# A step's norm transposes and projections moved one step earlier, and the rotation with them

## What is computed

```
xn  = layernorm(x)
out = x + attn(xn) + ffn(xn)
attn: q, k, v = xn @ Wqkv; q and k rotated by position (16 heads of 8); scores plus a bias that
      falls with |i-j| (per head); causal softmax; times v; @ Wo
ffn:  n1 = layernorm(xn, w, b); rw = gating(n1)              (8 experts, at least 2 active)
      q, k, v = sum over e of rw[e] * (n1 @ proj[e]); causal softmax attention
      hs = xn + sum over e of rw[e] * (attention @ o_proj[e])
      n2 = layernorm(hs); rw2 = gating(n2)
      hs + sum over e of rw2[e] * (gelu(n2 @ w1[e]) @ w2[e])
```

## Time and profile before

| what | us |
|---|---|
| median of three runs | 1389.92 |
| the three runs | 1386.5 to 1391.0 |
| the profiled execution | 1386.97 |
| its span in the trace | 1385.1 |

### The profile page before, as it was taken

One profiled execution on the slowest core, in us unless ns is written; L12 is line 12 of the kernel. 1 busy time (PEld: TensorE's weight loads), 2 busy tenths in 40 slices (PEclk: granted clock), 3 DMA queues, 4 the chain that ended last, 5 costly groups with the idle time before them and its releaser, 6 DMA issues.

```text
span 1385.1 us, 33706 instructions
## 1 busy us (share of the span) xinstructions
PE 1229.1 (89%) x10780; PEld 938.4 (68%) x10780; DVE 1004.5 (73%) x3691; ACT 707.4 (51%) x1281; POOL 211.0 (15%) x325
## 2 busy tenths in 40 slices
PE   1249999999999999999999999999999979999998
PEld 0127777777777677777777777777777766777776
DVE  5547777777777777777777777777777657777653
ACT  1115555555555555555555555555555665555532
POOL 1011111121111222221111111112111200000000
PEclk9659999999999999999999999999999999999999
DMA  5312232222222222222322222222222106544344
GB/s 131 87 63 79 79 90 81 82 82 77 78 78 82 81 80 78 77 77 81 96 97 77 77 79 88 81 82 81 80 80 78 53 26 230 194 154 154 154 169 153
DMA packets 107942, 133.19 MB, mean 96 GB/s; under 512 B 18116, under 2 KB 87252, under 8 KB 99692
## 3 DMA queue, kind: packets, MB, share of 16 engines
q1 hardware_dynamic: 105668, 131.66, 29.6%
q10 hardware_dynamic: 2216, 0.80, 0.2%
HBM read 109.12 MB, written 21.54 MB: 94 GB/s over the span
## 4 chain that ended last, share of the span: by engine, by line
PE 68%; DVE 16%; issue 9%; SPq 4%; DMA 2%; ACT 1%; DVEq 0%; ACTq 0%
PE ps L1448 9%; PE ps L1493 9%; PE ps L1694 8%; PE ps L1449 8%; PE ps L1680 8%; PE ps L1321 4%; PE ps L1458 3%; PE ps L1425 2%; DVE mx L1070 2%; PE ps L1408 2%; SPq L415 2%; PE ps L1371 1%; PE ps L1507 1%; PE ps L1381 1%; DVE xn L894 1%
## 5 line engine op out<-in xcount | busy, mean ns | idle before, releaser
L1070 DVE TENSOR_REDUCE mx<-ps 128x4 f32<-128x1024 f32 (+1 forms) x192 | 234.9, 1223 | 89.4 <-PE ps L1381 80.0
L663 ACT ACTIVATE pr<-ps 128x1024 f32<-128x1024 f32 x192 | 195.8, 1020 | 138.4 <-PE ps L1408 93.7
L558 POOL TENSOR_TENSOR n1s<-rep,n1T 128x256 f32<-128x256 f32 x256 | 176.8, 728 | 254.3 <-DVE mpart L1084 254.3
L669 ACT ACTIVATE ps<-trn 128x1024 f32<-128x1024 bf16 x191 | 197.2, 1032 | 5.1
L1694 PEld LDWEIGHTS ps<-w2s,ats 128*128 128x128 f32 x1024 | 131.7, 192 | 49.8 <-issue 46.8
L1448 PE MATMUL ps<-n1s,wqk 128*128 128x256 f32 x512 | 163.0, 400 | 0.0
L1449 PE MATMUL ps<-n1s,wqk 128*128 128x256 f32 x512 | 152.7, 380 | 0.0
L1458 PE MATMUL ps<-wv,n1s 128*128 128x128 f32 x1024 | 141.6, 281 | 0.0
L1493 PE MATMUL ps<-wop,ats 128*128 128x128 f32 x1024 | 140.0, 294 | 0.0
L842 ACT ACTIVATE n1s<-ps 128x512 f32<-128x512 f32 x128 | 76.5, 597 | 122.6 <-PE ps L1680 121.5
L1694 PE MATMUL ps<-w2s,ats 128*128 128x128 f32 x1024 | 135.7, 276 | 0.5 <-DVE ats L1253 0.5
(11 more groups left out here) (228 smaller groups left out, 2038.3 us busy)
## 6 DMA issues: line engine op xcount, KB each, us to landing
rep<-scr_rw SPq DMA_DIRECT2D x32, 1024.0 KB, 5.0
stk<-scr_rw SPq DMA_DIRECT2D x16, 1024.0 KB, 8.1
stk<-scr_parts SPq DMA_DIRECT2D x896, 16.0 KB
scr_parts<-parts SPq DMA_DIRECT2D x64, 192.0 KB, 2.3
rots<-scr_rw SPq DMA_DIRECT2D x8, 1024.0 KB, 4.8
wqk<-scr_rw SPq DMA_DIRECT2D x8, 1024.0 KB, 8.9
stk<-scr_parts SPq DMA_DIRECT2D x128, 48.0 KB
xt<-in_x SPq DMA_DIRECT2D x32, 128.0 KB, 2.5
```

The lines of the kernel that those rows point to most:

```text
L558: pool.tensor_tensor(n1s[:, e], rep[:, par, e], n1T[:, par], ALU.mult).then_inc(n1s_done, 1)
L663: act.activation(pr[:, Q, :, i], ps[:, S2[0]:S2[0] + NF], ACT.Exp).then_inc(exp_done, 1)
L669: act.activation(ps[:, S2[0]:S2[0] + NF], seeds[:, kind:kind + 1].broadcast_to((P, NF, 512)), ACT.Copy).then_inc(seed_done, 1)
L1070: dve.tensor_reduce(mx[:, min(i, 1)].rearrange("p (f h) -> p f h", f=NF)[:, :, h:h + n], ps[:, S1[0]:S1[0] + NF].rearrange("p f (h t) -> p ...
```

## The change

Sequence n+3 instead of n+2 now gets its norm transposes, both projections and its rotation in step n, in the step's tail; sequence n+2's gating stays in step n. The transposes go into S1[0] (after the last `row_max`), the q projection into S1[1], the k projection into PVB (after `add_x` has read it). `weights_T` and `max_T` move to G1. On PE `unit1`(2) to `unit1`(5) each move one place forward. On DVE `rotate` stands between `add_x` and `add_hs`, and all six `row_max` stand beside gating links. On ACT `evac_norm` is split: xnT in the tail, n1T and its square at the head of the next step.

```diff
-GATE_MAX_AT = (7, 12, 17, 22)
+GATE_MAX_AT = (2, 7, 11, 16, 20, 24)
...
+        FIRST, LATER = (G0, G1, G1), (S1[0], S1[1], PVB)
...  ACT, step
                 if n_x >= 2:
-                    evac_norm(n + 2, u)
+                    evac_norm_1(n + 2, u, LATER)
...
                 if n_x >= 2:
+                    evac_v(n + 2, u)
+                if n_x == 3:
+                    evac_norm_x(n + 3, LATER)
+                if n_x >= 2:
                     evac_weights(n + 2)
-                    evac_v(n + 2, u)
...  DVE, step
                 def beside_gating(k):
                     next(norm, None)
                     if k in GATE_MAX_AT:
-                        next_max(2 + GATE_MAX_AT.index(k))
-                    if k == 11:
+                        next_max(GATE_MAX_AT.index(k))
+                    if k == 17:
+                        soft_max(n)
+                    if k == 18:
                         normalise(n, 0)
-                    if k == 14:
-                        soft_max(n)
-                    if k == 20:
+                    if k == 28:
                         soft_norm(n)
                 if n_x >= 2:
-                    rotate(n + 2, beside_rotation)
-                    next_max(1)
                     gating(n + 2, T, 0, gate1, LG1, NORM1, 1, beside_gating)
...
                 add_x(n, u)
+                if n_x == 3:
+                    rotate(n + 3, LATER)
                 add_hs(n, u)
...  PE, step
-                if n_x >= 2:
-                    norm_T(f, lambda: pe.wait_ge(ats_done, len(ATS_CHUNKS) * n))
                 unit2(n, u, 0)
                 qk(n, 0)
-                if n_x >= 2:
-                    proj(f, 0, lambda: pe.wait_ge(hs_done, n))
                 qk(n, 1)
...
                 if n_x >= 2:
-                    proj(f, 1, lambda: pe.wait_ge(rot_chain, ROT_LINKS * f + 1))
                     logits(f)
...
                 qk(n, 6)
+                next_max(2)
                 qk(n, 7)
-                pv(n, u, 0)
+                pv(n, u, 0, f if n_x >= 2 else None)
...
                 if n_x >= 2:
-                    weights_T(f, True)
                     proj_v(f, True)
+                if n_x == 3:
+                    norm_T(g, LATER, lambda: pe.wait_ge(s1_read, UNITS * f))
+                    proj(g, 0, LATER, lambda: None)
+                if n_x >= 2:
+                    weights_T(f, lambda: None)
                 if n_x:
                     max_T(n + 1)
                 att_T(n)
+                if n_x >= 2:
+                    pe.wait_ge(rwT_done, f + 1)
+                if n_x:
+                    pe.wait_ge(mT_done, n + 2)
                 oe(n, 0)
                 oe(n, 1)
                 att_out(n)
+                oe(n, 2)
+                oe(n, 3)
+                if n_x == 3:
+                    proj(g, 1, LATER, lambda: pe.wait_ge(xa_done, n + 1))
...
-                for e in range(2, E):
+                for e in range(4, E):
                     oe(n, e)
```

More of the change, by code:

```diff
@@ L609, in _, with evac_norm_x, evac_norm_1 @@
             act.activation(red[:], red[:], ACT.Sin).then_inc(set_act, 1)
-            def evac_norm(b, par):
+            def evac_norm_x(b, banks):
+                act.wait_ge(xzT_out, b + 1)
+                act.activation(xnT[:], ps[:, banks[0], 0:S], ACT.Copy).then_inc(xnT_done, 1)
+            def evac_norm_1(b, par, banks):
                 act.wait_ge(xzT_out, b + 1)
@@ L616, in evac_norm @@
                     act.wait_ge(n1s_done, E * (b - 1))
-                act.activation(xnT[:], ps[:, G0, 0:S], ACT.Copy).then_inc(xnT_done, 1)
-                act.activation(n1T[:, par], ps[:, G0, S:2 * S], ACT.Identity, bias=lnp[:, 1:2],
+                act.activation(n1T[:, par], ps[:, banks[0], S:2 * S], ACT.Identity, bias=lnp[:, 1:2],
                                scale=lnp[:, 0:1]).then_inc(n1T_done, 1)
@@ L813, in _ @@
             for b in range(2):
-                evac_norm(b, b)
+                evac_norm_x(b, FIRST)
+                evac_norm_1(b, b, FIRST)
                 evac_logits(b)
@@ L1312, in norm_T, with proj @@
                     for i in range(T):
-                        ins = pe.transpose(ps[:, G0, (T * k + i) * P:(T * k + i + 1) * P], src[:, i], ident[:])
+                        ins = pe.transpose(ps[:, banks[0], (T * k + i) * P:(T * k + i + 1) * P], src[:, i], ident[:])
                 ins.then_inc(xzT_out, 1)
-            def proj(b, side, prev):
+            def proj(b, side, banks, prev):
                 pe.wait_ge(xnT_done, b + 1)
@@ L1320, in proj @@
                 for k in range(2):
-                    ins = mm(ps[:, G1, k * S:(k + 1) * S], wa[:, 2 * side + k], xnT[:], start=True, stop=True)
+                    ins = mm(ps[:, banks[1 + side], k * S:(k + 1) * S], wa[:, 2 * side + k], xnT[:], start=True, stop=True)
                 ins.then_inc((rot_q_out, rot_k_out)[side], 1)
@@ L1345, in proj_v, with weights_T, unit1 @@
                 ins.then_inc(v_out, 1)
-            def weights_T(b, old):
+            def weights_T(b, free):
                 pe.wait_ge(rw_out, 3 * (b + 1))
[L1349 to L1354, removed]
+                free()
+                pe.transpose(ps[0:E * T, G1, 0:P], gt[:, 6, 0:T].rearrange("p i e -> p (i e)"), ident[:]
                              ).then_inc(rwT_out, 1)
-            def unit1(b, par, k):
+            def unit1(b, par, k, front=None):
                 Q, i = divmod(k, 3)
-                if k == 0:
-                    pe.wait_ge(rwT_done, b + 1 if not isinstance(b, int) or b else 2)
-                    pe.wait_ge(mT_done, b)
+                if k == 0 and front is not None:
+                    pe.wait_ge(n1T_done, front + 1)
+                    pe.wait_ge(rot_chain, ROT_LINKS * front + 1)
                 if i == 0:
@@ L1413, in unit2, with pv @@
                 ins.then_inc(s2_out, 1)
-            def pv(n, u, Q):
+            def pv(n, u, Q, front=None):
                 pe.wait_ge(exp_done, UNITS * n + 3 * (Q + 1))
@@ L1422, in pv @@
                     pe.wait_ge(xa_done, n)
+                    if front is not None:
+                        pe.wait_ge(rot_chain, ROT_LINKS * front + 3)
                 for f in range(NF):
@@ L1461, in ve, with soft_scores @@
                     ins.then_inc(ve_out, 1)
-            def soft_scores(n, free):
+            def soft_scores(n):
                 pe.wait_ge(qkT_done, 2 * (n + 1))
-                free()
+                pe.wait_ge(hs_done, n)
                 b = ps[:, G1]
@@ L1593, in step @@
                 qk(n, 6)
+                next_max(2)
                 qk(n, 7)
-                pv(n, u, 0)
+                pv(n, u, 0, f if n_x >= 2 else None)
                 if n_x == 0:
                     logits2(0)
-                next_max(2)
+                next_max(3)
                 unit2(n, u, 3)
-                soft_scores(n, (lambda: pe.wait_ge(rot_chain, ROT_LINKS * f + 3)) if n_x >= 2 else
-                            (lambda: pe.wait_ge(hs_done, n)))
+                soft_scores(n)
                 ve(n, 0)
```

52 lines of the change are left out of this document (28 added, 24 removed).

## The result

The changed kernel takes 1460.18 us at the median of four runs (1449.65 to 1475.48), the kernel before 1389.76: slower by a ratio of 1.0485, interval 1.0385 to 1.0585. The forecast was 1442 with a range of 1402 to 1464. The ratio is that of the other three runs, since the profiled execution, 1475.48, is over 1.5% longer than the shortest.

The account below looks back on a forecast made before the run. TensorE's queue was taken to set the pace. A step loses 4.3 us instead of 3.05, plus 0.1: 28 x 1.3 = 36; 1387 + 36 + 19 for the clock = 1442 us, range 1402 to 1464.

Parts of the forecast that it names:

- The main term: TensorE at unit1(1) loses 2.8 us a step through the late load of xt; u is the start of unit2(0).
- the loop: unit1(1), k projection, rotation, hs, bs, load of xt, statistics, row_max(0), unit1(1) again; nothing in it overlaps.
- What it takes away: TensorE's waits at weights_T, max_T, att_T, unit1(5) and nearly all of soft_T's go: up to 3.05 us a step.
- What it adds in the tail: Losses at the q projection (0.6), pv(1) (0.55), oe(0) (0.25) and soft_T (0.1): together 1.5 us a step.
- The rival with the early load: Load of xt isn't last, there when the gating starts: a step 0.95 us shorter, 1353 us; chance 0.11.
- The clock: TensorE's clock falls in three of four steps instead of nine of 28: 12 more falls at 1.55, 19 us.
- The landing: Load of xt, 128 KB, lands 2.5 us after issue by the trace, 2.3 by the Trainium skill; 2.5 used.

Follow-up runs that it names:

- The early load: Changed kernel with the load of xt for sequence n+3 issued at the head of SP's step, ahead of its wait for base_done: 1368.02 us, ratio 0.985.
- the swap: Changed kernel with xt's load ahead of xr's in SP's step, both still behind base_done: 1412.63 us, ratio 1.0179 to the kernel before.
- the place of the rotation: Changed kernel with the rotation behind add_hs instead of right behind add_x, SP's order unchanged: 1413.4 us, ratio 1.0165 to the kernel before.
- the place of row_max(0): Changed kernel, late load kept, with row_max(0) ahead of the layer norm's first piece: 1372.56 us, ratio 0.9887 to the kernel before.
- the run that fills it: Changed kernel with six extra unused 128x256 float matmuls in front of unit1(1): 1430.64 us, ratio 1.0294 to the kernel before.

## Why the prediction was right, and where it was off

The direction, the mechanism and the place were right, and the median lies inside the range, near its upper end. Of the 18 us by which it misses the forecast, 3 are the base (the prediction starts from the profiled 1387, not from the median) and 13 the short steps, if these are as long in the executions that have no trace. That leaves 2 for the clock, so the size of the miss is that of one term in the tail.

- *The main term.* u + 3.0 for base_done was measured as u + 3.0, the statistics at u + 6.7 (predicted 7.0), TensorE due at unit1(1) at u + 6.4 (6.4), started at u + 9.1 (9.2). The loss there was 2.6 to 2.9 (2.8) in the short steps. The early load, the swap, the place of the rotation and the place of row_max(0) each move it as the loop says.
- *What it takes away.* Right: nothing waits at weights_T, at max_T or for the softmax any more.
- *What it adds in the tail.* The q projection, 0.64 (0.6), and pv(1), 0.63 (0.55), were right. The first oe was mis-sized: 0.83 to 0.88, not 0.25. The step that failed is "oe(0) waits for ScalarE's mT, some 0.7 behind max_T, with 0.2 and 0.3 of work in front". ScalarE copies the weights first, and by the change that copy waits for max_T too (mT_out, since both lie in bank G1), so two copies stand in a row behind it:

```profile
847.66 0.27 ACT L649 ACTIVATE rwT<-ps 16x128 f32<-16x128 f32 x1 [1.52 <-PE ps L1396]
847.84 0.36 ACT L654 ACTIVATE mT<-ps 48x256 bf16<-48x256 bf16 x1
```

  The first oe starts 848.43 - 847.27 = 1.16 behind max_T, not 0.7: the copy of the weights is 0.18 of the difference, and 0.23 from the end of mT's copy to the start of oe had been left out. The work in front is 0.33 (max_T 0.11, att_T 0.22), not 0.5. With this term a step loses 4.85 instead of 4.3, and 28 x 1.75 = 49 took the place of 36.
- *The rival with the early load.* For the case that the load isn't last I had a step 0.95 shorter than before. The kernel with the early load shows none: 3.2 lost instead of 2.1, by the 0.6 at the first oe and because unit1(1) loses 0.94, not 0.6. What it gains comes from the clock: its steps average 0.57 less than before (some 16 of the 21 us), and the nine falls had cost 0.5 a step. That rival's 1353 would have been 1368.
- *The clock.* Three of four steps were forecast and 20 of 28 measured. No row of the kernel before gave three of four, so that the number came out is luck. The size did not, in the profiled execution: 1.55 for each was taken from the steps before, where the clock was low for 3.4 us; here it was low for 6.8 in twelve steps, and a long step is 2.8 above the short ones on the mean. Forecast for the clock: 19. Measured there: 20 x 2.8 less the 15 of before, 41, of which some 9 are late landings (an estimate from the step lengths above). With 49 for the short kind that makes 90, and the spans differ by 88.6. The medians differ by 70.4, which leaves some 21 beside the 49, close to the 19: that the total is near is in part this, since the median run had less of the low clock than the profiled one.
- *The landing.* The page of the profile shows 2.5 again for xt, and the mean idle in front of the statistics is 2.2 (predicted 2.2), but that is a mean of two kinds: on time it is 1.6 to 2.1 (2.4 from issue to statistics in the step shown), in thirteen of 28 steps 2.4 to 3.0. The prediction counted with one value in every step; the spread matters because each late landing went with a fall of the clock. The 2.3 by the Trainium skill (DMA: Bandwidth & Descriptors, "Anatomy of one DMA — SWDGE (gpsimd) path") and the trace's 2.5 could not be told apart by the total, beside the clock.

That the clock falls more often and for longer was shown to come from TensorE's wait at unit1(1) by the run that fills it. Of the twelve falls of 6.8 us, eleven are in steps with a late landing; of the eight of 3.4 us, two. Why of two steps with the same wait (2.5 to 2.8) one has a fall and the other none stays open, and so does why the load issued second lands late at times.

## What to carry to other kernels

When a step moves, look at what counts up behind it: here the rotation was put in front of two small sums whose semaphore releases a load on another engine's queue, and the load's 6.6 us of room went with it. A load should wait for its own buffer to be free and for nothing else; here it stood behind a semaphore that it did not need. In a queue in order put what others wait for ahead of what itself may wait: moving one row maximum ahead of the layer norm took 88 us off with the load as late as ever. And a median of landings hides a spread: look at the slowest of them where an engine waits for each.

## What was not expected of the hardware

- A stall of TensorE can cost more than its length. Waits of 1.8 to 2.2 at unit1(1) were followed by a low clock of 3.4 us in 8 and 12 of 28 steps (the swapped loads, the rotation last), and these steps are 1.7 to 1.8 above the rest; waits of 2.4 to 3.8 in 20 of 28, with steps up to 3.9 above. Waits of up to 1.8 at unit1(2), with row_max(0) first, were followed by none.
- Of two loads of 128 KB issued one behind the other, 0.6 to 0.7 us apart, the second landed late at times: xt 2.9 us or more from issue to use in 13 of 28 steps behind xr, in none when it was issued first.
- 2.75 us of matmuls that nobody uses, put in the wait, made the kernel 30 us faster.
